# Input-norm statistics of chunks 2 and on: ScalarE in two passes in place of VectorE

## The reference

```python
x = L0_attn_x                                  # (8, 1024, 256)
h = _layernorm(_layernorm(x), ln_g, ln_b)      # mean and variance over the 256 numbers of a row, twice
xz = h @ W_in                                  # x_in and z, 512 wide each
x_c = silu(causal_depthwise_conv(x_in, conv_w, conv_b))
dt, Bm, Cm = split(x_c @ W_xproj)
delta = softplus(dt @ W_dt + b_dt)
s = exp(delta * A) * s + delta * B * x_c       # 16 states for each of 512 channels, step by step
y = (sum over states of s * C + x_c * D) * silu(z)
x = x + _layernorm(x) + y @ W_out
# then: layer norm, router, 2 of 8 experts for each row, residual, layer norm
```

## Time and profile before

| | |
|---|---|
| three runs | 2350.8 us (median), 2343.01, 2351.16 |
| profiled execution | 2349.51 us, its span 2348.0 us |
| mean granted TensorE clock | 0.973 of full speed |
| busy share of the span | PE 92%, DVE 87%, POOL 82%, ACT 71% |
| Mamba loop, chunks | about 110 us for each of 16 |

### The profile page before, as it was taken

How to read it: one execution, slowest core, us unless ns; L and a number is a source line. 1 busy time by engine, 2 the same in 40 slices (tenths; PEclk the granted TensorE clock), 3 DMA queues, 4 the chain that set the end, 5 groups by cost and what they waited for, 6 DMA issues and landing times. The chain is left out here.

```text
span 2348.0 us, 45628 instructions
## 1 busy us (share of the span) xinstructions
PE 2161.2 (92%) x13383; PEld 1741.0 (74%) x13383; DVE 2038.7 (87%) x2843; ACT 1661.8 (71%) x3402; POOL 1916.6 (82%) x1207
## 2 busy tenths in 40 slices
PE   8889899999999898989898989999978999999995
PEld 5667777767667776767777776776767889999885
DVE  5899999999999999899999999999999456647776
ACT  6686878778787878777778786877775444445664
POOL 3887989898988989888889898989898466667775
PEclk9999999999999999999999999999998999999998
DMA  6041414232232415050514141313235667657886
GB/s 186 2 154 49 142 51 148 66 125 97 94 121 70 157 43 170 21 170 23 170 33 158 52 144 58 138 65 126 77 105 165 140 112 152 139 96 163 182 181 147
DMA packets 226007, 263.60 MB, mean 112 GB/s; under 512 B 101123, under 2 KB 182563, under 8 KB 225636
## 3 DMA queue, kind: packets, MB, share of 16 engines
q1 hardware_dynamic: 175172, 208.07, 28.8%
q0 software_dynamic: 29904, 34.77, 8.1%
q10 hardware_dynamic: 20688, 17.85, 2.5%
HBM read 196.75 MB, written 71.71 MB: 114 GB/s over the span
## 5 line engine op out<-in xcount | busy, mean ns | idle before, releaser
L893 POOL TENSOR_TENSOR dbu<-drive_u,w_all 128x1024 f32<-128x1024 f32 x384 | 904.2, 2363 | 101.3 <-DVE ps_a L754 46.5
L1172 ACT ACTIVATE ps_a<-delta,a_neg 128x512 f32<-128x512 f32 x768 | 517.2, 685 | 141.1 <-DVE area L754 124.4
L910 POOL TENSOR_TENSOR wp<-area 128x1024 f32<-128x1024 f32 x192 | 453.0, 2359 | 36.8 <-DVE area L754 36.2
L766 DVE TENSOR_TENSOR wd<-ps_a,area 128x1024 f32<-128x1024 f32 x320 | 384.5, 1202 | 0.0
L1436 PEld LDWEIGHTS ps_y<-ident,wd 128*128 128x128 f32 x2560 | 302.5, 144 | 100.0 <-issue 71.1
L1436 PE MATMUL ps_y<-ident,wd 128*128 128x128 f32 x2560 | 341.3, 279 | 13.3 <-DVE wd L766 13.2
L2010 POOL DMA_INDIRECT acc_scratch<-ow,e_meta x135 | 221.7, 1642 | 138.6 <-DVE ow L1928 126.9
L1463 PEld LDWEIGHTS ps_a<-dg,duT 128*128 128x128 f32 x2048 | 252.6, 199 | 67.4 <-issue 64.8
L1463 PE MATMUL ps_a<-dg,duT 128*128 128x128 f32 x2048 | 262.7, 283 | 38.9 <-ACT carry L1179 36.3
L2239 PEld LDWEIGHTS e_ps_h<-xT,w_tile 128*128 128x128 f32 x2160 | 261.4, 193 | 19.6 <-DVE xT L1906 10.1
L2239 PE MATMUL e_ps_h<-xT,w_tile 128*128 128x128 f32 x2160 | 267.4, 277 | 5.2 <-issue 2.9
(11 more groups left out here) (245 smaller groups left out, 3772.0 us busy)
## 6 DMA issues: line engine op xcount, KB each, us to landing
area<-b_scratch SPq DMA_DIRECT2D x128, 512.0 KB, 4.7
w_all<-b_scratch SPq DMA_DIRECT2D x96, 512.0 KB, 4.0
dg<-xs_scratch SPq DMA_DIRECT2D x540, 32.0 KB
area<-in_L_attn_x_dram SPq DMA_DIRECT2D x32, 512.0 KB, 5.0
ee<-acc_scratch SPq DMA_DIRECT2D x32, 512.0 KB, 4.1
x_scratch<-area SPq DMA_DIRECT2D x16, 512.0 KB, 2.9
acc_scratch<-area SPq DMA_DIRECT2D x16, 512.0 KB
area<-x_scratch ACTq DMA_DIRECT2D x32, 256.0 KB
```

Of the source, the lines that this page charges most:

```text
L766: dve.tensor_tensor(wd[:, s % NWD], states(k, 2), cc[:, n:n + 2, :], ALU.mult).then_inc(wd_done, 1)
L893: pool.tensor_tensor(dbu[:, k % NBU], du[:, g % 2, :].unsqueeze(1).broadcast_to([P, 2, CH]), bb[:, row:row + 2, :], ALU.mult).then_inc(dbu ...
L910: pool.tensor_tensor(wp[:, s % 2], ss[:, s % 2], cc[:, rows, :], ALU.mult).then_inc(wp_done, 1)
L1172: act.activation(dst, dl[:, g, :], ACT.Exp, scale=a_neg[:, g, n:n + 1]).then_inc(exp_done, 1)
```

## The change

The statistics of chunks 2 to 15 move from VectorE to ScalarE. Chunks 0 and 1, which are handled ahead of the loop, keep VectorE's. In place of four `bn_stats` and four `bn_aggr` on VectorE there are four `Copy` of a 128x256 tile of `xb` onto itself, with a row sum (steps 46 and 47, two each), one small multiplication by -1/D that gives minus the mean (step 48, in place of that in step 51), and four `Square` of `xb` less the mean, with a row sum (steps 49 and 50, two each; they write to `hx`). `sums` and `sqs` are tiles that the second norm uses as well. The calls stand behind silu and ahead of `inv_std` in each step.

```diff
-        STATS = (47, 48)
+        STATS = (46, 47, 48, 49, 50)
...
-                for j, offset in enumerate(STATS):
-                    q = due(at, offset, 2)
-                    if q is not None:
-                        (stats_a, stats_b)[j](q)
...
+            def stats(q, step):
+
+                before = 4 + 3 * (q - 2)
+                if step < 2:
+                    if step == 0:
+                        act.wait_ge(x_in, 16 * (q + 1))
+                        act.wait_ge(lnr_step, 2 * (q - 2))
+                    for i in range(2 * step, 2 * step + 2):
+                        ins = act.activation(xb[:, i, :], xb[:, i, :], ACT.Copy, accum_out=sums[:, i:i + 1])
+                    if step == 1:
+                        ins.then_inc(ln_step, 1)
+                elif step == 2:
+                    act.wait_ge(ln_step, before + 1)
+                    act.wait_ge(prm, q)
+                    act.mul(nm[:, 0, :], sums[:], -1.0 / D).then_inc(ln_step, 1)
+                else:
+                    if step == 3:
+                        act.wait_ge(ln_step, before + 2)
+                        act.wait_ge(proj_full, full("h", 1, q - 1))
+                        if q > 2:
+                            act.wait_ge(x1_out, 16 * (q - 2))
+                            act.wait_ge(xn_done, q - 2)
+                    for i in range(2 * (step - 3), 2 * (step - 3) + 2):
+                        ins = act.activation(hx[:, i, :], xb[:, i, :], ACT.Square, bias=nm[:, 0, i:i + 1],
+                                             accum_out=sqs[:, i:i + 1])
+                    if step == 4:
+                        ins.then_inc(ln_step, 1)
+
             def inv_std(q, step):
 
                 r = q % 3
-                if step == 0:
+                if step == 0 and q > 1:
+                    act.wait_ge(ln_step, 4 + 3 * (q - 1))
+                    act.activation(pw[:, 0, :], sqs[:], ACT.Ln, bias=eps[:, 0:1], scale=(1.0 + EPS) / D)
+                    act.activation(pw[:, 1, :], sqs[:], ACT.Ln, bias=eps[:, 1:2], scale=1.0 / D).then_inc(rs_done, 1)
+                elif step == 0:
...
+                for j, offset in enumerate(STATS):
+                    q = due(at, offset, 2)
+                    if q is not None:
+                        stats(q, j)
                 for j, offset in enumerate(INV_STD):
```

## The result

| | before | after |
|---|---|---|
| median | 2348.3 us (4 runs, 2343.01 to 2351.16) | 2376.06 us (4 runs, 2373.13 to 2379.62) |
| profiled execution, span | 2349.51, 2348.0 us | 2374.56, 2372.9 us |
| granted TensorE clock | 0.973 | 0.968 |

The ratio is 1.0125, with a 95% interval from 1.0107 to 1.0143: slower by 28 us, where 12 were forecast.

A forecast was written before the change was run, and what follows sets the result against it. TensorE's queue bounds up to `dt` of step 48, then VectorE and ScalarE together. Even chunks 6.8, odd 6.0, chunks 0 and 9 0.9, chunks 8 and 12 -1.5: +12 us, so 2362 us, range 2338 to 2385.

The forecast's parts named there:

- what bounds the kernel: TensorE's queue of projections sets the pace up to `dt` of step 48; then VectorE and ScalarE run side by side.
- the prices of the instructions: On ScalarE, 0.37 us for a `Copy` and 0.49 us for a `Square`; 3.44 us more a chunk in all.
- the copies and the wait for x cost nothing: Steps 46 and 47: ScalarE's idle stretches of 1.88 and 2.02 us cover them, with 1.1 us left at `dt`.
- x comes too late: Rival: ScalarE misses `dt`, so the copies are paid too, up to 3.44 us a chunk; 2398 us, chance 0.14.
- the squares are late for VectorE: Steps 49 and 50, after `dt`: nothing covers the squares; VectorE is late by 1.7 us in even chunks, 1.0 in odd.
- The odd ones out: Chunks 8 and 12 gain 0.8 and 0.7 us; chunk 0 loses 0.6 and chunk 9 0.3.
- Absorbed: Rival: VectorE's later stalls, about 4 to 6 us a chunk, take up the loss; time stays at 2350 us, chance 0.15.
- the term for even chunks: Chunks 2, 4, 6, 10: ScalarE 1.96 us late from step 51, less slack at step 54; 4 x 1.7 = 6.8 us.
- the slack at step 54: Even chunks: ScalarE's exponential of step 54 ends 0.3 us before VectorE's scan, less some 0.05 for the hand-over.
- an estimate of 0.3 us lost: Chunk 9: VectorE has other work of 1.97 us in step 49, so a loss of 0.3 us was estimated.
- The first rival: VectorE is the bound: the hole at step 48 closes and all 22.5 us are won; 2327 us, chance 0.13.

## Why the prediction was right and wrong

**Right: what bounds the kernel.** TensorE's queue up to `dt`, then VectorE and ScalarE side by side. With all statistics gone from VectorE the time fell by 0.3%, with VectorE's added again it did not rise.

In the Trainium skill, Perfetto Trace Analysis (Identifying the Most-Contended Engine) would relieve the engine with the highest occupancy first. The runs here disagree for VectorE: relief of 22.5 us that cost nothing won 6.5 of them. By that rule the change would have won 22 us.

**Right: the prices of the instructions.** A `Copy` with a sum from SBUF takes 0.42 us from start to start (795.84 to 796.26), between the 0.37 and 0.49 given; a `Square` 0.50 (803.02 to 803.52), forecast 0.49. The wait for x was forecast at 1.7 us (781.0 to 782.74) and is 1.6.

**Right: the copies and the wait for x cost nothing**, by the run without copies and by the one with x earlier. So the rival "x comes too late" falls. Of the 1.1 us that were to be left at `dt`, 0.89 are.

**Right: the squares are late for VectorE.** Odd chunks lose 1.03 us, forecast 1.0. Even ones had lost 1.49 by step 51, forecast 1.7 by step 54. The odd ones out: chunk 8 won 0.7 and chunk 12 1.2 (0.8 and 0.7 forecast), chunk 0 lost 1.4 (0.6). These terms sum to 12.6 us against 12. That the sums lie so close is partly luck: chunk 0 lost 0.8 us more than forecast and chunk 9 0.5, even chunks 0.2 each less by step 51, and chunk 12 won 0.5 more. "Absorbed" falls too: from step 63 of one chunk to step 40 of the next the difference shrinks by no more than 0.7 us, and no later stall took it up.

**Wrong: the term for even chunks, "late by 1.96 less the slack at step 54 ...: 1.7 us".** It stopped at VectorE. In the same queue behind the squares stood the copy of the carried states, on which TensorE's drives wait, and ScalarE itself waits for these drives and for z. Both waits were in the trace before, 36.3 us in sum for the first and 0.26 us in chunk 6 for z, but the prediction followed neither; its "ScalarE is busy without a break until step 64" passes over the 0.26 us, and over 0.31 us for GpSimd. In chunk 6 the squares lengthened TensorE's idle time from 2.90 to 4.08 us. Its granted clock, which before had been at 0.60 for one window, then stayed near 0.5 for two, and drives and z took 3.75 and 3.18 us in place of 3.04 and 2.56. ScalarE waited for both, and VectorE for ScalarE. Chunks 2, 4, 6 and 10 so lost 1.9 to 3.1 us each. That the drives' wait is the origin is shown by the run with the carry in step 49: the growth of steps 51 to 63 falls from 8.5 us to 2.4, and chunk 6 then loses 1.48 + 0.24 = 1.7 us, as forecast. So the slack at step 54 was right, and some 6 us of TensorE's were missing. Their size is partly chance: with the same late carry the run with x earlier has 5.8 us in this row, which leaves 3.4, and the difference lies in the chunks in which z too met the lower clock.

**Wrong: chunk 9, "an estimate of 0.3 us lost".** It lost 3.2: 0.78 by step 51, and 2.41 in one instruction. VectorE after:

```profile
1156.62 2.64 DVE L700 TENSOR_TENSOR early_jump<-early_passed,early_jump 128x8 f32<-128x8 f32 x1
1159.18 1.27 DVE L754 TENSOR_TENSOR_SCAN ps_a<-dbu,carry,ps_a 128x512 f32<-128x512 f32 x1
```

GpSimd in the same stretch:

```profile
1155.63 2.36 POOL L906 TENSOR_TENSOR wp<-area 128x1024 f32<-128x1024 f32 x1
1157.94 1.28 POOL L876 TENSOR_TENSOR drive_u<-delta,xc 128x512 f32<-128x512 f32 x1
```

The same L700 took 0.23 us before:

```profile
1136.18 0.23 DVE L700 TENSOR_TENSOR early_jump<-early_passed,early_jump 128x8 f32<-128x8 f32 x1
```

After, it began in the middle of GpSimd's instruction and ended with the one that follows; before, it began 0.2 us ahead of the end of that instruction. In the run with the earlier carry it took 2.08 us, and chunk 9 lost 1.85 there, just the difference to 0.23. All 13 profiles fit: in eight it began 0.2 us ahead of that end and took 0.22 to 0.24 us; in the other five, those with the squares behind `dt`, it began 0.5 to 1.4 us ahead, took 1.75 to 2.64 us, and ended within 0.04 us of GpSimd's second instruction. That GpSimd's instructions are what holds it is still read from their times alone; no run took them away.

The Trainium skill has a rule for this: by SBUF — State Buffer, section Who interferes with whom, an instruction of VectorE with two inputs in SBUF and one of GpSimd that reads SBUF exclude each other, and the later one waits for the whole of the other. These times agree with it; at 2.64 us the wait went on into a second instruction of GpSimd.

**Wrong by omission: the clock under `dbc`.** The balance of steps 40 to 43, 6.2 us, comes from stretches of lower clock while TensorE is the bound. They come and go between executions of the same program (6.5 us less in the repeated one), so a part of this row is chance. But in chunks 0 to 14 they are seven to ten in the four profiles with the squares behind `dt` and the carry late, six with the earlier carry, and one to five in the eight without late squares (the two of before among them). Why late squares bring them, some 90 us further on, stays open.

**The first rival, VectorE the bound,** falls with the run without statistics: 0.9970 and not 0.99.

## What to carry to other kernels

Work moved to an engine with idle time is priced by the place in its queue: the same eight activations cost 3 us in front of the wait for `dt`, 28 behind it, and 37 where they delayed what TensorE waits for. List everything that stands behind the insertion in the queue, down to a 0.14 us copy, and who waits for each. Where TensorE is one of those who wait, look also at the granted clock at which it then works: the same two groups took 3.9 to 6.9 us here. Work that fills a hole ahead of a wait, as the `bn_stats` did here, is not worth removing.

## What was not expected of the hardware

- TensorE's drives and z took 2.02 and 1.88 us after 2.91 us of idle time in chunk 4 before, but 3.04 and 2.56 after 2.90 us in chunk 6 before. After 4.08 us (chunk 6 after) they took 3.75 and 3.18, with a granted clock near 0.5 over some 7 us; after 4.73 (chunk 4 of the run with x earlier) 3.39 and 1.88. The length of the idle time alone did not decide the pace.
- The clock also fell for about 3.4 us at a time in stretches where TensorE was busy throughout, at places that differ between two executions of one program; each cost 1.5 to 1.7 us, and together they made 6.5 us between two profiles.
- An operation of VectorE on 128x8 took 0.23, 2.08 or 2.64 us (chunk 9: before, after with the earlier carry, after), and in all 13 profiles this went with where in GpSimd's instructions it began.
